# Making both halves of a scan's inputs with one GpSimd instruction

## What is computed

```python
delta = softplus(xc @ Wd.T + bd)          # 512 tokens x 256 channels
Bm, Cm = xc @ Wb.T, xc @ Wc.T             # 512 tokens x 16 states
A = -exp(log_a)                           # 256 channels x 16 states
def step(h, inputs):                      # over the 512 tokens
    dt, bt, ct, xt_ = inputs
    decay = exp(A[None] * dt[:, :, None])
    inp = dt[:, :, None] * xt_[:, :, None] * bt[:, None, :]
    h = decay * h + inp
    y = einsum('bdn,bn->bd', h, ct)
```

## Time and profile before

| | before |
|---|---|
| median of the runs | 1981.06 us |
| lowest and highest | 1978.12, 1986.54 us |
| the profiled execution | 1986.2 us |
| its span, first to last instruction | 1984.4 us |
| PE (TensorE) busy | 1749.4 us, 88% |
| DVE (VectorE) busy | 1719.0 us, 87% |
| ACT (ScalarE) busy | 1411.7 us, 71% |
| POOL (GpSimd) busy | 1182.6 us, 60% |

### The profile page before, as it was taken

The page is one execution under the profiler, slowest core; times in us unless marked ns, Lnnn a source line. Parts: engine busy times, 40 slices in busy tenths (PEclk is TensorE's granted clock), DMA queues, the critical chain, the costliest instruction groups (busy, mean ns, idle before and its releaser), DMA issues.

```text
span 1984.4 us, 32798 instructions
## 1 busy us (share of the span) xinstructions
PE 1749.4 (88%) x10311; PEld 1053.3 (53%) x10356; DVE 1719.0 (87%) x3928; ACT 1411.7 (71%) x2724; POOL 1182.6 (60%) x933
## 2 busy tenths in 40 slices
PE   5999788989899898999899898989999898778875
PEld 2555454646465565646465564646565464535333
DVE  5654889998999999899999999899999989977893
ACT  3667668687877868687877868787877868664641
POOL 2001666667767676667767666657667655776530
PEclk9999899999999999999999999999999999998987
DMA  4321676878677786877777776877777777651110
GB/s 139 92 77 48 139 158 142 171 153 173 143 158 168 155 182 145 172 158 166 144 159 170 153 178 148 173 155 163 153 164 162 151 163 146 141 116 54 49 59 11
DMA packets 186094, 275.37 MB, mean 139 GB/s; under 512 B 33809, under 2 KB 125762, under 8 KB 185922
## 3 DMA queue, kind: packets, MB, share of 16 engines
q1 hardware_dynamic: 155682, 163.17, 33.4%
q0 software_dynamic: 30240, 110.11, 29.8%
HBM read 128.49 MB, written 34.08 MB: 82 GB/s over the span
## 4 chain that ended last, share of the span: by engine, by line
PE 25%; DMA 21%; DVE 20%; POOL 12%; issue 11%; ACT 9%; SPq 2%; POOLq 0%; DVEq 0%; ACTq 0%
DMA y<-hc 14%; PE bank L421 7%; DVE hc L1259 6%; DVE bank L1116 5%; POOL inp L1434 4%; POOL inp L1428 4%; PE bank L627 3%; DVE hc L1267 2%; DMA X<-in_x 2%; PE bank L482 2%; DMA sk<-qk_parts 2%; PE bank L504 2%; POOL rs L1406 2%; PE bank L610 2%; PE bank L529 2%
## 5 line engine op out<-in xcount | busy, mean ns | idle before, releaser
L1259 DVE TENSOR_TENSOR_SCAN hc<-dec,inp 128x1024 f32<-128x1024 f32 x256 | 631.3, 2471 | 28.2 <-ACT dec L1017 14.4
L1428 POOL TENSOR_TENSOR inp<-u,b_all 128x512 f32<-128x512 f32 x256 | 428.7, 1675 | 197.1 <-DVE hc L1259 116.8
L1116 DVE CUSTOM_DVE_ANT_0 bank<-bank,mask_qk 128x512 f32<-128x512 f32 (+3 forms) x1024 | 477.9, 508 | 72.2 <-PE bank L482 71.3
L901 ACT ACTIVATE pt<-bank 128x512 f32<-128x512 f32 x640 | 378.0, 596 | 175.9 <-PE bank L506 173.5
L1434 POOL TENSOR_TENSOR inp<-u,b_all 128x512 f32<-128x512 f32 x240 | 409.3, 1705 | 18.8
L1017 ACT ACTIVATE dec<-dt,a_neg 128x511 f32<-128x511 f32 x512 | 339.6, 717 | 48.9 <-DVE hc L1259 48.8
L1441 POOL DMA_DIRECT2D y<-hc x210 | 185.0, 881 | 314.8 <-DMA y<-hc 234.4
L504 PE MATMUL bank<-sq,sk 98*128 98x512 bf16 (+3 forms) x1024 | 275.8, 308 | 44.9 <-ACT pt L901 42.9
L1267 DVE TENSOR_TENSOR hc<-hc,bank 128x1024 f32<-128x1024 f32 x242 | 293.4, 1212 | 19.7 <-PE bank L664 19.1
L482 PE MATMUL bank<-sk,sq 96*128 96x512 bf16 (+3 forms) x1024 | 251.9, 308 | 44.8 <-DVE mall L1116 26.2
L506 PE MATMUL bank<-mask_kq,ident_bf 128*128 128x128 bf16 x1024 | 197.2, 224 | 0.0
(11 more groups left out here) (167 smaller groups left out, 3118.8 us busy)
## 6 DMA issues: line engine op xcount, KB each, us to landing
y<-hc POOLq DMA_DIRECT2D x210, 512.0 KB, 5.2
b_all<-b_kept SPq DMA_DIRECT2D x256, 256.0 KB, 4.0
qk_parts<-parts SPq DMA_DIRECT2D x96, 256.0 KB, 2.9
sq<-qk_parts SPq DMA_DIRECT2D x384, 64.0 KB, 4.0
sk<-qk_parts SPq DMA_DIRECT2D x384, 64.0 KB, 4.1
X<-in_x SPq DMA_DIRECT2D x16, 512.0 KB, 7.8
out<-X SPq DMA_DIRECT2D x16, 512.0 KB, 4.6
sq<-hlt SPq DMA_DIRECT2D x256, 2.0 KB
```

Of the source, the lines that this page charges most:

```text
L901: A(pt[:, n % PT, :], score_bank[unit % 2][:, :], ACT.Exp).then_inc(exp_done.sem, 1)
L1116: return V.tensor_tensor_reduce(src[:, o:o + n], src[:, o:o + n], mask_qk[:, T - n:T], 1.0, -3.0e38, ALU.add, ALU.max, out)
L1259: V.tensor_tensor_scan(h, d, v, 0.0, ALU.mult, ALU.add).then_inc(scan_done.sem, 1)
L1428: first = G.tensor_tensor(inp[:, n % 2, 0, :], u[:, 0, :], b_all[:, k % 3, :], ALU.mult)
```

## The change

The two instructions of 128x512 become one of 128x1024. Its output is both halves of `inp`, its first operand both halves of `u`, and its second operand the row of `b_all`, read twice (a broadcast over the halves). The signal and the wait on `pool_own` between the halves go. The last batch keeps its single half. Order, buffers and all other waits stay.

```diff
                 behind()
-                first = G.tensor_tensor(inp[:, n % 2, 0, :], u[:, 0, :], b_all[:, k % 3, :], ALU.mult)
                 if s == NB - 1:
-                    first.then_inc(inp_ready.sem, 1)
+                    G.tensor_tensor(inp[:, n % 2, 0, :], u[:, 0, :], b_all[:, k % 3, :],
+                                    ALU.mult).then_inc(inp_ready.sem, 1)
                 else:
-                    first.then_inc(pool_own.sem, 1)
-                    pool.wait_ge(pool_own.sem, pool_own.one())
-                    G.tensor_tensor(inp[:, n % 2, 1, :], u[:, 1, :], b_all[:, k % 3, :], ALU.mult).then_inc(inp_ready.sem, 1)
+                    G.tensor_tensor(inp[:, n % 2, :, :], u[:, :, :],
+                                    b_all[:, k % 3, None, :].to_broadcast([P, C, T]),
+                                    ALU.mult).then_inc(inp_ready.sem, 1)
                 ends(inp_ready, s, n + 1)
```

## The result

The changed kernel takes 2052.47 us (median of four runs, 2046.51 to 2055.38); the kernel before, on the same chips, 1979.59. The ratio is 1.036, with a 95% interval from 1.0331 to 1.0389: 73 us slower. The forecast was 2015 us, in a range up to 2042. The direction was right; the size was half of what came, and the time lies outside the range.

The account below looks back on a forecast made before the run. The prediction took VectorE (DVE) to set the pace. Longer waits of +37.7 us, less 4.2 us from earlier inputs at first steps, gave +33.5 us on the 1981.1 us median: 2015 us, range 1974 to 2042.

Parts of the forecast that it names:

- What bounds the kernel: Step claiming VectorE sets the pace, busy 104.92 of 112.00 us in a middle batch, while POOL has 34 us idle.
- Price of the single instruction: Step estimating 128x1024 on POOL from the times of 512 and 4 elements: 2.35 us, upper bound 2.54.
- What lets a scan in: Claim that scan and POOL instruction exclude one another; a waiting scan got in at the seam between POOL's halves.
- A: Scan of step 4, 12 times, waiting 1.03 us: 1.08 us more less 0.40 cover, 8.2 us in all.
- B: Scan of step 10, 12 times, waiting 1.88 us: 1.08 us more each, no cover, 13.0 us in all.
- C: Scan of step 13, 10 times, waiting 0.35 us: 1.08 us more each, no cover, 10.8 us in all.
- D: Scan six us after C, 10 times, waiting 0.08 us: the wait goes, giving back 0.8 us.
- What a scan loses: Step listing scans that wait for a first half today and adding their longer waits: 37.7 us in all.
- Case 1: Rival: phases fall anew and meetings of scans and POOL may thin out; 1986 to 1999 us, chance 0.18.
- Case 4: Rival: more meetings, D stays, A has no cover, the instruction takes 2.54 us; 2047 us, chance 0.07.
- Case 2: Rival: POOL was on the path at A, so its earlier end makes the kernel faster; 1951 us, chance 0.12.
- Case 3: Rival: the single instruction lets a scan in half-way, so scans wait as before; 1972 to 1977 us, chance 0.08.

Follow-up runs that it names:

- e5: Changed kernel with the product u * b left out, GpSimd filling inp twice with a constant in all batches but the last: 1962.23 us, ratio 0.989.
- e1: Kernel before, both halves of 128x512 kept, but the second no longer waits for the first: 2060.79 us, ratio 1.040.
- e12: Kernel before with the single instruction in step 5 alone, the pair in the 15 other steps: 2025.44 us, ratio 1.021.
- e13: Kernel before with the single instruction in step 11 alone, the pair in the other steps: 1996.69 us, ratio 1.007.
- e3: Changed kernel plus four waits on POOL, holding back its inputs of steps 5, 6, 11 and 14 behind VectorE instructions: 2027.49 us, ratio 1.023.
- e4: Kernel before, with its pair, plus the same four waits on POOL as in e3: 2016.54 us, ratio 1.016.

## Why the prediction fell short

- **What bounds the kernel.** That VectorE sets the pace held in the direction that mattered: 6.3 us more of waits, 6.3 us longer batches. It was not the whole: without any port waits (e5) a batch still takes 110.0 us. The forecast needed only the first.
- **Price of the single instruction.** 2.35 us estimated, 2.338 the shortest measured. The rule of two rows and a slope was enough.
- **What lets a scan in.** "Got in at the seam between the halves" held, and e1 made it exact: the wait is the seam, not the boundary between two instructions.
- **A.** Forecast 1.08 - 0.40 for cover. The wait rose by 0.8 (the scan also came 0.25 us later into POOL's instruction), and there was no cover: the idle time before the product, 0.4 us in the earlier trace rows, was up to 3 us after the change, that at the load of x lower, and the sum per batch went from 6.9 to 7.2. In the changed kernel's chain the product at 713.31 waits for TensorE, and the work before it goes back over PE and ScalarE to VectorE's own product, which ended at 701.42; idle time that begins on VectorE moves with it and covers nothing. Why this one grew isn't shown. In e12 A rose by 1.09.
- **B.** 1.08 forecast, 1.08 measured, and e13 shows its price on the clock: 14 us.
- **C and D.** D went, as forecast. So did C in most batches, which wasn't; silu, 1.9 us ahead of it on VectorE, met POOL's instruction instead. So the 10.8 us that the sum has for C didn't come there, and that the forecast got as far as 34 is in part luck: A and B alone, the terms that held, are 21.
- **The step that failed** is the list under "What a scan loses". It took the VectorE instructions that wait today, and counted how much longer they would wait. It should have taken all that *can* wait, every instruction with two inputs in SBUF, with the margin by which each is ahead of POOL now. lg was ahead by 0.44 us, less than the 1.08 us by which the text itself moved VectorE. silu was ahead by 0.23 us, less than the 0.28 us by which the text made POOL's free step shorter; it put that saving into POOL's idle time, at no cost. At those two it would have said: if passed, up to 2.35 us, and for lg some 0.4 us more, while POOL issues the add of y. lg grew by 35 us and silu by 16, 51 us of the 88, and with the scan of step 8 (11 us) they are what was missed.
- **The rivals.** Case 1 asked whether phases fall anew and saw only that they might thin out; they fell anew and thickened. Case 4 had nearly the right size (2047) for other reasons: a D that stays, an instruction of 2.54 us. Case 2, POOL on the path, is out: at A the chain of waits ran over POOL, POOL's end there came earlier, and the kernel got slower. Case 3 is out: scans wait up to 3 us for one instruction.
- **What stays open.** e12 and e13 account for 42 + 14 = 56 of the 73 us. That silu, whose waits grew by 16 us, makes up the rest is likely, but no run has the single instruction in steps 13 and 14 alone. Why the scan of step 8 waits more often isn't shown. Why holding POOL back costs 2 us of idle time a batch (e3, e4) wasn't followed up; in the trace what rose most from the changed kernel to e3 is the idle time before the score maxima, which wait for TensorE (from 0.7 to 2.3 us a batch). No version here that still makes the product u * b beats the kernel before by more than the measurement can tell.

## What to carry to other kernels

When two engines exclude one another, list every instruction that could lose, not those that lose now, with its margin; a change that moves either engine against the other by more than a margin, by making one late or the other early, can buy a whole new wait, and its price is the length of the other engine's instruction, even for 24 elements. A wait on one's own semaphore between two instructions can be worth keeping: between these two halves it was the only place where the other engine got in. And an engine with idle time (POOL, 30%) isn't worth making faster if the busy one pays for it.

## What the runs showed of the hardware

- Two GpSimd instructions queued back to back hold VectorE's two-input instruction out as one of double length would: 4.37 us for a scan in e1, against 3.31 with a wait of 0.08 us between them. I had thought that any end of an instruction lets the other engine in. The Trainium skill (SBUF — State Buffer, section Who interferes with whom) says that a VectorE instruction with two SBUF inputs contends with a GpSimd instruction that reads SBUF, and, of VectorE's two-port modes, that whoever issues first gets the shared ports for the whole instruction. The runs agree for a scan and 1024 elements on GpSimd too (the scan at 687.11, 4.10 us), and add that the next one in GpSimd's queue can follow without letting go.
- A VectorE instruction that starts while GpSimd is still issuing a DMA can also lose, to the tensor instruction queued behind that DMA: the scan at 1173.79, lg at 693.79 after the change. In both the VectorE instruction starts 0.2 to 0.4 us before GpSimd's tensor instruction shows in the trace, and still comes second. It isn't so each time: in the changed kernel the scans of step 8 at 370.30 and 723.75 started 0.35 us into an add's issue, 0.32 and 0.46 us before the tensor instruction, and took 2.29 us, while that at 840.98, 0.27 us before it, took 5.08. What decides isn't shown.
- GpSimd instructions that only write kept no scan waiting in any middle batch (e5, mean 2290 ns over 256 scans).
